# Two expert products placed among the Horner tiles of a graph-ODE and mixture-of-experts kernel

## The reference

```
h = layernorm(x) @ fc_in_w.T + fc_in_b          # x0 = layernorm(x)
8 times: h = h + (1/8) * (alph*0.5*(adj @ h - h) + h @ w_eff - h + x0)
x = x + h
z = layernorm(x)
combine = renormalised top-2 of softmax(z @ router_w.T)     # 8 experts
x = x + z + sum over e of combine[:, e] * (gelu(z @ w1[e] + b1[e]) @ w2[e] + b2[e])
```

## Time and profile before

| what | value |
|---|---|
| median of 3 runs | 532.05 us |
| the profiled execution | 531.63 us |
| its span | 529.5 us |
| TensorE busy | 514.8 us (97%) |
| VectorE busy | 439.4 us (83%) |
| ScalarE busy | 297.8 us (56%) |
| GpSimd busy | 112.8 us (21%) |
| loop iterations 1 to 6 | 355.07 us in all |

### The profile page before, as it was taken

One profiled execution on the slowest core, in us unless ns is written; L12 is line 12 of the kernel. 1 busy time (PEld: TensorE's weight loads), 2 busy tenths in 40 slices (PEclk: granted clock), 3 DMA queues, 4 the chain that ended last, 5 costly groups with the idle time before them and its releaser, 6 DMA issues.

```text
span 529.5 us, 9181 instructions
## 1 busy us (share of the span) xinstructions
PE 514.8 (97%) x2799; PEld 451.0 (85%) x2799; DVE 439.4 (83%) x1012; ACT 297.8 (56%) x533; POOL 112.8 (21%) x174
## 2 busy tenths in 40 slices
PE   5999999999999999999999999999999999999996
PEld 4687997997799888998899878988799888997775
DVE  6798777789967997789967997789977996589896
ACT  6324433449625884459535883459535882149584
POOL 1204004213150412212240412222240412021010
PEclk9999999999999999999999999999999999999999
DMA  4040011099326972198327962298327951161071
GB/s 133 2 119 1 0 41 40 27 269 225 61 59 146 287 141 61 45 264 209 59 59 175 265 137 59 59 275 188 55 59 196 242 99 20 45 228 49 2 239 41
DMA packets 139359, 62.04 MB, mean 117 GB/s; under 512 B 102614, under 2 KB 133964, under 8 KB 137420
## 3 DMA queue, kind: packets, MB, share of 16 engines
q1 hardware_dynamic: 139340, 61.81, 46.5%
HBM read 47.90 MB, written 13.89 MB: 117 GB/s over the span
## 4 chain that ended last, share of the span: by engine, by line
PE 83%; DVE 7%; DMA 3%; ACT 2%; issue 2%; SPq 2%; POOL 1%; DVEq 0%; ACTq 0%; POOLq 0%
PE bank L1126 21%; PE bank L1128 21%; PE bank L1127 20%; PE bank L1303 11%; PE bank L1310 6%; DMA x0q<-x_rows 2%; PE bank L1252 1%; DVE scs L670 1%; DVE bn L674 1%; DMA x_rows<-x 1%; ACT work L604 1%; DVE work L982 1%; SPq L338 1%; DVE Q L1094 1%; PE bank L1154 1%
## 5 line engine op out<-in xcount | busy, mean ns | idle before, releaser
L670 DVE TENSOR_TENSOR scs<-work,scs 128x512 fp32r<-128x512 f32 x132 | 98.6, 748 | 1.7 <-ACT scs L481 0.5
L604 ACT ACTIVATE work<-bank,cols 128x512 f32<-128x512 f32 x128 | 86.7, 678 | 16.0 <-PE bank L1128 15.8
L481 ACT ACTIVATE scs<-work 128x512 fp32r<-128x512 f32 x132 | 83.1, 630 | 20.4 <-DVE work L982 19.0
L1303 PE MATMUL bank<-scs,w2s 128*128 128x512 f32 x256 | 80.7, 396 | 0.0
L1128 PE MATMUL bank<-M,GT 128*128 128x384 f32 x192 | 64.2, 335 | 0.0
L1126 PE MATMUL bank<-M,GT 128*128 128x384 f32 x192 | 64.2, 334 | 0.0
L1127 PE MATMUL bank<-M,GT 128*128 128x384 f32 x192 | 64.2, 334 | 0.0
L982 DVE TENSOR_TENSOR work<-work,GT 128x512 f32<-128x512 f32 x90 | 60.9, 683 | 1.7 <-ACT work L604 0.9
L422 POOL TENSOR_TENSOR mv<-bn 128x8 f32<-128x8 f32 x16 | 6.9, 429 | 239.5 <-DVE bn L674 239.5
L1303 PEld LDWEIGHTS bank<-scs,w2s 128*128 128x128 f32 x256 | 47.7, 188 | 10.7
L481 ACT ACTIVATE GT<-bank 128x512 fp32r<-128x512 f32 x36 | 21.1, 595 | 58.3 <-PE bank L1128 55.7
(11 more groups left out here) (196 smaller groups left out, 1220.5 us busy)
## 6 DMA issues: line engine op xcount, KB each, us to landing
GT<-comb_rows SPq DMA_DIRECT2D x8, 1536.0 KB, 7.0
Q<-comb_rows SPq DMA_DIRECT2D x16, 512.0 KB, 7.1
GT<-comb_rows SPq DMA_DIRECT2D x7, 1024.0 KB, 5.7
xn<-in_x_dram SPq DMA_DIRECT2D x16, 256.0 KB, 4.0
GT<-comb_rows SPq DMA_DIRECT2D x7, 512.0 KB, 4.2
res_rows<-scr SPq DMA_DIRECT2D x12, 256.0 KB, 2.6
x_rows<-x SPq DMA_DIRECT2D x12, 256.0 KB, 2.6
x0q<-x_rows SPq DMA_DIRECT2D x24, 128.0 KB, 3.9
```

Of the source, the lines that this page charges most:

```text
L481: return nc.scalar.activation(dst, src, ACT.Copy)
L604: nc.scalar.activation(hid[:, i % 2, :], bank[UP_BANK[i % 3]][:, :], ACT.Gelu, bias=cols[:, B1_COL + e:B1_COL + e + 1]).then_inc(gelu_done, 1)
L670: return v.tensor_tensor(dst, src, hi.bitcast(FP32), ALU.subtract)
L1303: pe.matmul(bank[SUM_BANK[b]][:, :], w2s[:, k, e, :], scs[:, i % RING, 0, :], start=(e == 0 and k == 0), stop=False)
```

## The change

For loop iterations alone, the up products of items 0 and 1 are issued among the Horner tiles: item 0 ahead of result t = 2 of the last part, item 1 ahead of t = 3. They go to banks 2 and 3, which the Horner tiles don't use, and all up products of the loop now rotate through banks 2, 3 and 4, not 4, 5 and 6. VectorE scales item 0 behind the statistics of result 0, ahead of the addition for result 2. TensorE waits for the last Gelu before the next node product uses banks 3 and 2. Iteration 7 and the last experts stay as they were. No instruction with arithmetic is added or taken away.

```diff
--- before.py
+++ after.py
@@ -224,7 +224,7 @@
         Z_SCALE, Z_AT = 5, [8, 10]
         BY_PE = GROUPS - 2
         ROUTE_AT = [0, 1, 3, 4]
-        UP_BANK, SUM_BANK = [4, 5, 6], [0, 1]
+        UP_BANK, UP_LOOP, SUM_BANK = [4, 5, 6], [2, 3, 4], [0, 1]
         X0_BANK, X0_SETUP = [2, 5], [6, 7]
         CREP_BANK, FR_BANK, V2_BANK = [1, 0, 3], [0, 2, 7], 0
         ZT_FIRST = [7, 6]
@@ -601,7 +601,7 @@
                     if i >= 2:
                         act.wait_ge(sc_ready, ITEMS * h + i - 1)
                     e = i % E
-                    nc.scalar.activation(hid[:, i % 2, :], bank[UP_BANK[i % 3]][:, :], ACT.Gelu,
+                    nc.scalar.activation(hid[:, i % 2, :], bank[(UP_LOOP if more else UP_BANK)[i % 3]][:, :], ACT.Gelu,
                                          bias=cols[:, B1_COL + e:B1_COL + e + 1]).then_inc(gelu_done, 1)
                     if i == 1 and g is None:
                         copy_comb(h)
@@ -991,7 +991,8 @@
 
 
                 for i in range(ITEMS):
-                    scale_item(h, i, g is None and i < REP_PE)
+                    if i >= 1 or not more:
+                        scale_item(h, i, g is None and i < REP_PE)
                     if i == 0 and g is None:
                         add_out(h - 1, 1)
                     if i >= 1:
@@ -1095,6 +1096,8 @@
                                     Q[:, 0, t], ALU.add).then_inc(x1_add, 1)
                     if t >= 1:
                         x1_stats(t - 1)
+                    if t == 1 and not first and not final:
+                        scale_item(g - 1, 0, False)
                 x1_stats(NT - 1)
                 if first:
                     for b in range(GB):
@@ -1275,16 +1278,23 @@
                                      pick[:, half, i:i + 1].to_broadcast([P, P]), combT[:, :], start=True, stop=True)
                 last.then_inc(rep_mm, 1)
 
+            def early_up(s):
+
+                mm3(bank[UP_LOOP[s]][:, :], w1s[:, 0, s, :], w1s[:, 1, s, :],
+                    zT[:, 0, 0, :], zT[:, 1, 0, :], True, True).then_inc(up_mm, 1)
+
             def experts(h, g=None, more=False):
 
                 for s in range(ITEMS + LAG):
-                    if s < ITEMS:
+                    if s < ITEMS and not (more and s < 2):
                         b, e = s // E, s % E
                         if s >= 3:
                             pe.wait_ge(gelu_done, ITEMS * h + s - 2)
+                        elif more:
+                            pe.wait_ge(x1_add, NT * g + 1)
                         elif g is not None:
                             pe.wait_ge(x1_add, NT * g + s + 1)
-                        mm3(bank[UP_BANK[s % 3]][:, :], w1s[:, 0, e, :], w1s[:, 1, e, :],
+                        mm3(bank[(UP_LOOP if more else UP_BANK)[s % 3]][:, :], w1s[:, 0, e, :], w1s[:, 1, e, :],
                             zt_part(0, b, g is None), zt_part(1, b, g is None), True, True).then_inc(up_mm, 1)
                         if s == 1 and g is None:
                             transpose_out(h - 1, 1)
@@ -1322,6 +1332,7 @@
                         if s < ITEMS + NT:
                             nodes_product_tile(0, s - ITEMS)
                 if more:
+                    pe.wait_ge(gelu_done, ITEMS * h + ITEMS)
                     nodes_product(1)
                     nodes_product(2)
                     logits(g)
@@ -1356,9 +1367,10 @@
                         pe.wait_ge(q_ready, T * g + NT + t + 1)
                 if not first:
                     pe.wait_ge(ct_high, g)
-                for _ in horner(y1s, H8_BANK, h8_mm, y1_lo,
-                                [((0,), NT * g + 1), ((1,), NT * g + 2), ((2, 3), NT * g + 4)]):
-                    pass
+                for tiles, t in horner(y1s, H8_BANK, h8_mm, y1_lo,
+                                       [((0,), NT * g + 1), ((1,), NT * g + 2), ((2, 3), NT * g + 4)]):
+                    if tiles[0] == 2 and t >= 2 and not first and not final:
+                        early_up(t - 2)
                 if first:
                     pe.wait_ge(x0_ready, g + 2)
                     transpose_x0(0)
```

## The result

Six runs of the changed kernel gave a median of 555.93 us (555.65 to 558.99), against 532.1 us (531.63 to 532.19, six runs) before. The ratio is 1.0467 [1.045, 1.0483]: the change costs 24 us, not 5.

What follows compares the result with a forecast made beforehand. VectorE at item 11 was taken to bound the loop, its time set by z, which waits for GpSimd's chain. Six iterations of 60.06 us, 360.36 against 355.07, gave 532.05 + 5.3 = 537.3 us, range 534.4 to 539.4.

Steps and rivals of the forecast that it cites:

- length of the chain: GpSimd's small statistic instructions ahead of z: 6.81 us as in iteration 5, less some 0.15 for running alone at the end.
- start of z: VectorE reaches z at 14.49 us of the iteration, waits for GpSimd and starts z at 15.30.
- low part 11: VectorE's low part of item 11 still collides with GpSimd's addition, 1.79 us; 0.7 us there would show the forecast wrong.
- Where the end is set: Loop iteration: everything from z to item 11 keeps its distances, so length is start of z plus 44.76 us.
- What TensorE's half costs: Two up products among the Horner tiles finish result 3 1.38 us later, delaying GpSimd's chain; TensorE's total is unchanged.
- So I cost this wait at nothing: result 3 hides it: VectorE's early scaling of item 0, waiting for Gelu 0, is through before result 3 at 7.34 us: no cost.
- 6.81 is the nearer row: GpSimd's chain takes iteration 5's 6.81 us, not iteration 2's 6.48, since VectorE goes straight from statistics into an item.
- Six iterations of one length: All six loop iterations near 60.06 us, since the backlog that told iteration 5 from iteration 2 is gone.
- TensorE's waits: No long step at up product 5; TensorE waits about 0.7 us at up product 12 and 0.7 at item 11.
- B: GpSimd's chain is quick (3.97 us) and VectorE reaches z unhindered: no change, +0.4 us, 532.5 us; chance 0.08.
- C: GpSimd's addition falls behind low part 11, so the collision at item 11 goes: -1.3 us, 530.7 us; chance 0.06.
- D: Early products and scaling wait for something else among the Horner tiles: up to another 1 us an iteration; chance 0.04.

Runs made afterwards that it cites:

- pe_only: Changed kernel with VectorE's list as before: early up products stay, item 0's scaling goes back behind all statistics; 538.83 us, 1.0131.
- low_psum: Changed kernel whose loop low parts subtract a PSUM bank in place of the high part (wrong results, measurement only); 528.81 us, 0.993.
- sem_before: Changed kernel in which VectorE's scaling of item 1 waits on a semaphore until Gelu 2 is done; 535.61 us, 1.0062.
- sem_gap: Changed kernel in which VectorE's low part 0 waits on a semaphore until ScalarE's high part 1 is written; 537.29 us, 1.0102.
- one_gap: Changed kernel with one short VectorE instruction (sum over eight SBUF values) added behind the scaling of item 1; 558.03 us, 1.0492.
- late_add: Kernel before, with GpSimd's first residual addition of an iteration held until the last low part is done; 530.9 us, 0.9978.
- wide_gap: Changed kernel with four short VectorE instructions (sums over eight SBUF values) added behind the scaling of item 1; 557.17 us, 1.0463.

## Why the prediction was wrong

Its direction was right and its path too; its size was wrong by 18.6 us (555.93 against 537.3), far above the range. Step by step, in iteration 2:

| step | forecast | kernel after |
|---|---|---|
| scaling of item 0 starts | near 6.0 | 6.02 |
| addition of result 3 | 7.34 | 7.35 |
| GpSimd's chain starts | 8.61 | 8.62 |
| VectorE ready for z | 14.49 | 14.55 |
| length of the chain | 6.65 | 9.61 |
| start of z | 15.30 | 18.27 |
| iteration = z + 44.76 | 60.06 | 63.03 |
| low part 11 | collides | collides, 1.79 us |

- **Where the end is set: right.** 18.27 + 44.76 = 63.03, the measured length. A relation read from a difference of 0.31 us between two iterations held at more than ten times that distance, and in pe_only (15.44, 60.20) too. It ends where the collision ends: low_psum had z at 14.44 and took 58.63 us, not 59.20.
- **What TensorE's half costs: right.** pe_only took 538.83 us, within the forecast's own range.
- **The failed step: "So I cost this wait at nothing: result 3 hides it", with "6.81 is the nearer row" for the chain.** The early scaling itself was hidden indeed: the addition of result 3 was on time. Its price lay elsewhere. In iteration 5 of before, too, GpSimd's first instruction missed its first chance: it lasted 1.18 us, from 354.48 to 355.66. Two scalings stood beside it, to 355.60, and behind them came VectorE's low part 0, in the trace of before:

```profile
355.69 0.69 DVE L670 TENSOR_TENSOR scs<-work,scs 128x512 fp32r<-128x512 f32 x1
```

  So GpSimd's instruction ended in a pause of 0.09 us, in which low part 0 waited for ScalarE. I read 1.18 as a slow start. I now read it as a wait for a pause; the row alone can't tell the pause from the end of the second scaling, but sem_before and sem_gap can, which keep the early scaling and give back a pause. The change removed it: item 0 was scaled early, its high part was written by the time low part 0 was due, and VectorE ran ten instructions without a break. What was missing was that pause, and not just a place for the first instruction: in one_gap the first one passed, and the second was held for 5.54 us. In the kernel after the chain took 6.00 us and 3.6 us alone behind it in place of 6.65 in all: 2.96 us an iteration, 17.8 us for six.
- **Six iterations of one length: nearly.** The three of 63.24 to 63.26 us and the three of 63.03 differ by the clock, below; that adds some 0.65 us.
- **TensorE's waits: of other sizes, and the first at another place.** No long step was left at up product 5, as forecast (in pe_only, where item 0 is scaled late, TensorE waited 1.06 us there). The waits were 2.84 and 0.28 us, not 0.7 and 0.7. The lateness of z arrives by way of Gelu 7, for which up product 10 waits, and not at up product 12 by way of Gelu 9. The length of the iteration does not hang on this.
- The sum closes: six iterations of 63.03 against a mean of 59.18 us (355.07 / 6) are +23.1, with 0.65 for the clock +23.75; the loop grew by 23.77.

**Rivals.** B (a quick chain) and C (no collision) did not come about in the kernel after. Nor did D: the scaling of item 0 started at 6.02, where it was forecast. The mechanisms of B and C exist, though. In low_psum the chain took 5.4 us and VectorE went into z unhindered at 14.44. In late_add the collision went, but in the kernel of before only 0.18 us an iteration of its 1.10 us came back (1.06 / 6): with z on time, item 11 bound the loop by little more than TensorE itself does.

**Open.** Why the chain passes at each end of a VectorE instruction once a semaphore's pause has let it in, while behind short instructions (one_gap, wide_gap) only one or two pass and the next is held, with the same spacing of 0.60 to 0.61 us on VectorE, is not shown. Nor is why pe_only's first instruction passed between two scalings that stood ready (0.58 us), where that of iteration 5 of before did not (1.18 us). The runs say only what served in every case tried: a pause that came from a semaphore.

## What to carry to other kernels

A short GpSimd chain that the critical path needs can live on pauses of VectorE that look like waste: before an edit makes VectorE's list "tighter", look in which pause each GpSimd instruction used to get in, and price the chain at the length of VectorE's unbroken row if that pause goes. A GpSimd instruction whose duration was several times its usual one was here a wait, not work, and its end told what it waited for. What got rid of it was a wait of VectorE's on a semaphore, of a few tenths of a microsecond. One operand read from PSUM did so too, but only in a kernel whose results it made wrong. Fill-in instructions and shifting the start did nothing.

## What the runs showed of the hardware that was not expected

- A GpSimd instruction of 0.21 us was held for 6.00 us beside ten, and for 8.41 us beside fourteen, VectorE instructions with two SBUF inputs (0.68 us each, one every 0.60 us). With one of the two inputs of every second instruction in PSUM it was held only to the end of the scaling beside it (0.58 us, low_psum).
- The hindrance is nearly one-sided in the rows: VectorE's 128x512 instructions took 0.67 to 0.70 us with a small GpSimd instruction waiting or passing, and 0.73 once an iteration in sem_before. GpSimd's 128x512 addition (1.58 us) cost VectorE 1.10 us on low part 11, and some 0.5 us on the scaling of item 12 in low_psum.
- After the wait of 2.84 us on TensorE in iteration 1 (ended at 130.13) the granted clock stood at 0.50 from 131 to 132, the lower level of 1.2 GHz; after the same wait in iteration 2 it didn't fall. It fell in iterations 1, 3 and 5, at about 0.2 us each.
